# Second weight copies of the mixed tiles in two buffers; group 14's output sum in PSUM tensor PC, added by VectorE after its last chain

## What is computed

```
xn  = layernorm(x)
mixer: x_proj, z = split(xn @ W_in.T);  xc = silu(causal conv over 4 taps + bias)
       dt = softplus(W_dt (W_x[32:] xc) + b_dt);  alpha = sigmoid(dt * 0.1)
       h[l] = clip(alpha) * h[l-1] + (1 - alpha) * B_gate * xc        (256 channels)
       mixer = ((h * C_gate + D * xc) * silu(z)) @ W_out.T
moe:   top 2 of 8 experts by xn @ w_gate, softmax over the two
       expert e: (silu(xn @ w1[e]) * (xn @ w3[e])) @ w2[e]
out = x + mixer + moe
```

## Time and profile before

| | |
|---|---|
| time before, median of 3 runs (lowest to highest) | 471.16 us (471.15 to 471.25) |
| time of the profiled execution | 471.31 us |
| its span | 469.6 us |
| PE, DVE, POOL, ACT busy | 430.6, 388.1, 310.6, 287.7 us |
| mean granted clock of PE | 0.993 |
| full tiles | up to about 371.6 us |
| mixed tiles 31 to 34, and tile 35 | about 371.6 to 405 us |
| tail | from about 405 us |

### The profile page before, as it was taken

One profiled execution on the slowest core, in us unless ns is written; L12 is line 12 of the kernel. 1 busy time (PEld: TensorE's weight loads), 2 busy tenths in 40 slices (PEclk: granted clock), 3 DMA queues, 4 the chain that ended last, 5 costly groups with the idle time before them and its releaser, 6 DMA issues.

```text
span 469.6 us, 8332 instructions
## 1 busy us (share of the span) xinstructions
PE 430.6 (92%) x2440; PEld 308.0 (66%) x2440; DVE 388.1 (83%) x774; ACT 287.7 (61%) x406; POOL 310.6 (66%) x344
## 2 busy tenths in 40 slices
PE   0888999999999999998999999999999878998877
PEld 0777544555554455555888888988988878664446
DVE  5885897999999999996998997677677675399985
ACT  2774469788888988898454434434434433668850
POOL 4677777777777775750677777777777777764200
PEclk9998999999999999999999999999999999999999
DMA  8961117131121312143677756666656652029994
GB/s 239 292 195 45 53 52 239 46 98 54 56 88 52 97 50 82 47 136 98 201 202 239 224 172 198 187 184 177 175 170 190 182 143 85 15 46 266 209 211 121
DMA packets 48077, 65.92 MB, mean 140 GB/s; under 512 B 8424, under 2 KB 30223, under 8 KB 48048
## 3 DMA queue, kind: packets, MB, share of 16 engines
q1 hardware_dynamic: 36240, 39.56, 30.2%
q0 software_dynamic: 10656, 24.47, 18.6%
q10 hardware_dynamic: 1152, 1.57, 1.2%
HBM read 42.09 MB, written 33.83 MB: 162 GB/s over the span
## 4 chain that ended last, share of the span: by engine, by line
PE 48%; DVE 29%; issue 13%; ACT 8%; DMA 1%; DVEq 0%; SPq 0%; ACTq 0%
PE PD L897 13%; DVE hbuf L1404 6%; PE PB L729 4%; DVE hbuf L1415 4%; PE PD L840 3%; PE PB L859 3%; PE PB L863 3%; PE PB L860 3%; PE PA L859 3%; DVE gbuf L1386 3%; PE PA L863 3%; PE PA L860 3%; DVE y L1424 2%; DVE gbuf L1292 2%; PE PC L744 2%
## 5 line engine op out<-in xcount | busy, mean ns | idle before, releaser
L612 POOL DMA_INDIRECT moe_out<-xnT,dst_u x142 | 146.6, 1033 | 61.7 <-issue 37.8
L597 POOL DMA_INDIRECT moe_in<-xn,slot_u x128 | 133.0, 1039 | 44.4 <-issue 39.9
L897 PE MATMUL PD<-xnT,xn 128*128 128x128 f32 x536 | 66.0, 276 | 1.3 <-DVE xn L1630 1.2
L897 PEld LDWEIGHTS PD<-xnT,xn 128*128 128x128 f32 x536 | 62.7, 192 | 2.4 <-DVE xn L1630 2.0
L744 PE MATMUL PC<-xc,Wc 128*128 128x512 f32 x128 | 57.8, 594 | 2.9 <-ACT xc L1102 2.9
L1176 ACT ACTIVATE whi<-xnT 128x512 fp32r<-128x512 f32 x36 | 22.8, 633 | 61.3 <-PE PB L863 61.3
L1205 ACT ACTIVATE xn<-PA 128x1024 f32<-128x1024 f32 (+1 forms) x36 | 36.5, 1013 | 34.4 <-PE PA L863 20.2
L757 PE MATMUL PA<-xnT,Wtap 128*128 (+4 forms) x128 | 57.2, 590 | 0.0
L1630 DVE TENSOR_TENSOR xn<-xn,PB 128x1024 f32<-128x1024 f32 (+1 forms) x36 | 43.4, 1207 | 11.1 <-PE PB L863 9.0
L1623 DVE TENSOR_TENSOR xlo<-PD,xhi 128x512 fp32r<-128x512 f32 (+1 forms) x36 | 24.6, 682 | 27.6 <-ACT xhi L1199 27.6
L757 PEld LDWEIGHTS PA<-xnT,Wtap 128*128 128x128 f32 x128 | 24.3, 190 | 30.5 <-issue 30.5
(11 more groups left out here) (246 smaller groups left out, 916.9 us busy)
## 6 DMA issues: line engine op xcount, KB each, us to landing
xnT<-moe_w SPq DMA_DIRECT2D x36, 256.0 KB
xn<-moe_in SPq DMA_DIRECT2D x31, 266.0 KB
out_dram<-moe_out POOLq DMA_DIRECT2D x12, 512.0 KB, 16.3
xnT<-moe_w SPq DMA_DIRECT2D x36, 128.0 KB
out_dram<-xacc SPq DMA_DIRECT2D x7, 512.0 KB, 3.5
moe_out<-xnT,dst_u POOLq DMA_INDIRECT x142
moe_in<-zrow SPq DMA_DIRECT2D x8, 266.0 KB, 3.4
moe_w<-in_L_ffn_w_dram SPq DMA_DIRECT2D x2, 1024.0 KB
```

The lines of the kernel that those rows point to most:

```text
L597: gp.indirect_dma_start(xs_dram, bass.IndirectOffsetOnAxis(ap=slot_u[:, k, j:j + 1], axis=0), xn_row[:, j, :], None).then_inc(s_scat, 16)
L612: gp.indirect_dma_start(yt_dram, bass.IndirectOffsetOnAxis(ap=dst_u[:, t, j:j + 1], axis=0), yo[t % OUTS][:, j, :], None, bounds_check=lim ...
L897: last = pe.matmul(PD[:, 512 + j * D:512 + (j + 1) * D], hid[b][:, k * SLOTS + j * P:k * SLOTS + (j + 1) * P], (w2x[t - FULL] if mixed and ...
```

## The change

`whix` and `wlox` get two buffers each, used in turn; `round_mixed` and `low_mixed` of the second mixed tile no longer wait, and those of the third and fourth wait for the PB matmuls of one tile earlier than before. On DVE `low_mixed(t+1)` stands ahead of `glu(t)` instead of behind it. In the tail, group 14's sums go to PC instead of PB: PE waits for `softplus(15)` (`s_dt`) instead of `add_out(15)` before them, the eight matmuls into PC and their wait are gone, and the wait before the last group's rows is for `add_out(15)` instead of `add_out(16)`. DVE's `add_out(16)` reads PC and stands behind the last chain part, ahead of the two last sums.

```diff
@@ -127,8 +127,8 @@
         wlo = sb("wlo", [P, 2, 2 * HID], F32R)
-        whix = sb("whix", [P, 2 * HID], F32R)
-        wlox = sb("wlox", [P, 2 * HID], F32R)
+        whix = sb("whix", [P, 2, 2 * HID], F32R)
+        wlox = sb("wlox", [P, 2, 2 * HID], F32R)
         xhi = sb("xhi", [P, 2, SLOTS], F32R)
@@ -868,7 +868,8 @@
                 pe.wait_ge(s_xhi, t + 1)
-                hi, lo = (whi[:, b, :], whix[:, :]), (wlo[:, b, :], wlox[:, :])
+                x = max(t - FULL, 0) % 2
+                hi, lo = (whi[:, b, :], whix[:, x, :]), (wlo[:, b, :], wlox[:, x, :])
                 pe.wait_ge(free, t)
@@ -959,21 +960,18 @@
             out(g, g % SLOT3, True)
-            pe.wait_ge(s_add, g)
             pe.wait_ge(s_rows, 16 * TOP_K)
-            pe.matmul(PB[:, 0:GROUP], ident[:, :], last_rows[0][:, 0:GROUP], start=True, stop=False)
-            pe.matmul(PB[:, 0:GROUP], ident[:, :], last_rows[1][:, 0:GROUP], start=False, stop=False)
+            pe.wait_ge(s_dt, GROUPS)
+            for c in range(TOP_K):
+                pe.matmul(PC[:, 0:GROUP], ident[:, :], last_rows[c][:, 0:GROUP], start=(c == 0), stop=False)
             pe.wait_ge(s_y2, g)
...
                 for k in range(HALVES):
-                    last = pe.matmul(PB[:, j * D:(j + 1) * D], gated_y(g)[:, k, j * P:(j + 1) * P], WoT[:, k, :],
+                    last = pe.matmul(PC[:, j * D:(j + 1) * D], gated_y(g)[:, k, j * P:(j + 1) * P], WoT[:, k, :],
                                      start=False, stop=(j == GT - 1 and k == HALVES - 1))
...
-            pe.wait_ge(s_ch, (GROUPS - 1) * CHAIN + 5)
-            for _ in range(8):
-                pe.matmul(PC[:, 0:P], ident[:, :], ident[:, :], start=True, stop=True)
-            pe.wait_ge(s_add, GROUPS)
+            pe.wait_ge(s_add, g)
             for h in range(2):
@@ -1178,9 +1176,9 @@
                 act.wait_ge(s_w13x[m], 16)
-                if m:
-                    act.wait_ge(s_h3, t)
-                act.activation(whix[:, :], w13x[m], ACT.Copy).then_inc(s_whix, 1)
+                if m > 1:
+                    act.wait_ge(s_h3, t - 1)
+                act.activation(whix[:, m % 2, :], w13x[m], ACT.Copy).then_inc(s_whix, 1)
@@ -1492,14 +1490,14 @@
-            def add_out(g, col=0):
+            def add_out(g, col=0, ps=PB):
...
                 at = bass.ds(g * GT - 2 * GT, GT) if not static else slice((g - 2) * GT, (g - 1) * GT)
-                ve.tensor_tensor(xacc[:, at, :], PB[:, col:col + GROUP].rearrange("p (j d) -> p j d", j=GT),
+                ve.tensor_tensor(xacc[:, at, :], ps[:, col:col + GROUP].rearrange("p (j d) -> p j d", j=GT),
                                  xacc[:, at, :], ALU.add).then_inc(s_add, 1)
@@ -1639,10 +1637,11 @@
             def low_mixed(t, b):
-                ve.wait_ge(s_whix, t - FULL + 1)
-                if t > FULL:
-                    ve.wait_ge(s_h3, t)
-                ve.tensor_tensor(wlox[:, :], w13x[t - FULL], whix[:, :].bitcast(F32), ALU.subtract).then_inc(s_wlox, 1)
+                m = t - FULL
+                ve.wait_ge(s_whix, m + 1)
+                if m > 1:
+                    ve.wait_ge(s_h3, t - 1)
+                ve.tensor_tensor(wlox[:, m % 2, :], w13x[m], whix[:, m % 2, :].bitcast(F32), ALU.subtract).then_inc(s_wlox, 1)
@@ -1703,9 +1702,9 @@
                     sum_p(t + 1, 1 - b, early and t == 0)
-                glu(t, b, early)
                 if isinstance(t, int) and is_mixed(t + 1):
                     low_mixed(t + 1, 1 - b)
+                glu(t, b, early)
@@ -1764,9 +1763,9 @@
             chain(g, slot, 2)
-            add_out(g)
             chain(g, slot, 3)
             chain(g, slot, 5)
+            add_out(g, 0, PC)
```

## The result

The changed kernel takes 466.76 us (median of 4 runs, 466.24 to 467.28) against 471.21 us (4 runs) for the kernel before: ratio 0.9907, 95% interval 0.9891 to 0.9923. It is faster by 4.4 us. The forecast was 464.5 us with a range up to 466.6; the time lies 2.3 us above the one and 0.2 us above the other. The profiled execution took 466.26 us, its span is 464.5 us.

What follows compares the result with a forecast made beforehand. PE, stopped for `wlox` in mixed tiles, and a tail chain mostly through DVE and ACT were taken as bounds; 471.31 - 5.7 (tiles) - 2.6 (tail) + 1.7 (slow clock) = 464.7, as median 464.5 us, range 462.9 to 466.6.

Steps and rivals of the forecast that it cites:

- What bounds: PE runs full tiles without a gap; each of four mixed tiles (6.55 us) stops 1.2 us for `wlox`; POOL late by itself.
- part 1: Mixed tiles: without the wait for `wlox` a tile takes 5.11 us instead of 6.55; 5.7 us saved, bounds 4.8 to 5.8.
- the ring through DVE and ACT: Mixed tiles: chain from one gate through xhi, `scale_y`, `wlox` and `glu` to the next, about 5.1 us, level with PE's 5.11.
- (b): Mixed tiles: DVE and ACT decide at 5.4 us a tile, or SP's row loads do; saving 4.7, total 465.5 us; chance 0.12.
- (d): Mixed tiles: the wait becomes an equal one for `glu` or `hid`, so only the tail's change works: 470.2 us; chance 0.05.
- (e): Tail: `add_out(14)` waits for the second transfer onto `xacc`, making it slower; landing at 450 gives 473.6 us; chance 0.03.
- Part 2: Tail, group 14 in PC: work starts 2.60 us earlier; PE's last 16 instructions at half clock take 1.7 us more.
- the 2.60: Tail: L1409 begins at 458.69 plus 0.03 instead of 461.32, since `add_out(16)` moves back: 2.60 us earlier.
- rival (a): Tail: PE's clock does not fall before the last matmuls, or only for the last few: 463.2 us; chance 0.17.
- forecast place: Tail: the last sum was to start at 465.95 - 5.7 = 460.25 us.
- Does something hold the tail?: Tail transfers: queue ends at 458 to 460, `add_out(14)` has 2.7 us of margin; no cost taken, bound 0 to 1.5 us.
- Rival (c): Kernel's end: final stores land up to 1.5 us late, or the queue ends at 462: 465.5 to 466.5 us; chance 0.11.

Runs made afterwards that it cites:

- two separate edits of POOL's end: Changed kernel with the last wait for the accumulating transfers on SP instead of POOL: 464.89 us; changed kernel without its last accumulating transfer: 464.79 us (both chip A).
- the changed kernel with SP's waits: Against the changed kernel, the last wait for the twelve accumulating transfers onto the output stands on SP, not POOL: 464.89 us, ratio 0.9871 (chip A).

## Why the prediction was wrong

**What bounds, and part 1: right.** The wait for `wlox` is gone, a tile takes 5.11 us as forecast, and the ring through DVE and ACT shows only as late gates on ACT. From tile 31's start to group 12's L744 it was 401.69 - 371.61 = 30.08 us and is 394.73 - 370.29 = 24.44: 5.64 us against the 5.7 taken. For comparison, the row of before:

```profile
401.69 1.88 PE L744 MATMUL PC<-xc,Wc 128*128 128x512 f32 x4
```

Rivals (b) and (d) fell with that. `add_out(14)` is at 439.6 and waits for no transfer: (e) fell too.

**Part 2: the mechanism right, its size taken from an execution whose clock fell.** L1407 stands straight behind the scan, `add_out(16)` costs nothing, PE idles 3.58 us (forecast 3.6). The forecast for this stretch was 15.50 - 2.60 + 1.7 = 14.6 us; it was 13.97, since the clock fell only within L984, which took 1.05 us more instead of 1.7. But the 2.60 held 1.7 us of slow clock of the old tail, and of six traces of the old tail only the profiled one has that. That does not make it rare: of the kernel before's eight executions on chip A two have the mean clock of the profiled one, 0.993, three have 0.996 and three 1.000. The prediction treated the fall as a property of the kernel; the runs show it in some executions of a kernel and not in others, and what rival (a) says of the clock holds in four of the new tail's nine traces. The Trainium skill, "TensorE: Matmul & The Clock Gate", section "HAM oscillation — how this bites in real kernels", has the burst behind each long wait begin cold; here, behind the same wait of 3.57 to 3.58 us, it was granted full speed throughout in four traces and 0.50 for most of it in five. The same holds at 36 us, where the profile of before fell and that of after did not: 1.3 us of their difference, ahead of all that was changed. So of the 1.9 us by which the last sum beat its forecast place, 1.3 came from the clock there and 0.6 from the clock in L984.

**The step that failed: "Does something hold the tail?"**, with "I take no cost, bound 0 to 1.5 us". It asked when POOL's queue would end and put that at 458 to 460 us, which is where it ended (458.5). It did not ask what POOL does then. Its DRAIN of 5.63 us stood in the trace of before, at 461.8, hidden by 1.9 us, and the forecast moved the computation's end by 5.7 + 2.6 - 1.7 = 6.6 us and POOL's queue by 2.5 at most. Measured, SP's end moved 8.2 us (469.3 to 461.1) and POOL's 3.2 (461.8 to 458.6), so 1.9 us of cover became 3.1 us of excess. From the prediction's own terms: 458 to 460, plus 5.63, plus 0.3 to the end of the span, is 463.9 to 465.9; with 1.7 around it 465.6 to 467.6 us. Measured 466.76. The last sum came 1.9 us earlier than forecast, but since POOL decides, the time does not show it.

Rival (c), "the transfers hold the end", named the right engine's work and by luck nearly the time (465.5 to 466.5), but through late stores or a queue that ends at 462, and neither happened: the last store landed 1.7 us after SP began to wait for it. That two separate edits of POOL's end give back 2.3 to 2.4 us shows the cause.

The cover of 1.9 us is that of the profiled execution: without its two falls of the clock the old kernel's last sum would come at about 466.85 - 1.3 - 1.7 = 463.9 and its span end at 466.6, an estimate, and two of its executions on chip A at clock 1.000 have spans of 467.1 and 467.5. POOL's DRAIN may have held those already; no trace here is of such an execution.

In the two profiled executions the account closes: the last sum is 8.50 us earlier (1.32 by the clock at 36 us, 5.64 by the tiles, 1.53 by the tail, 0.01 between), and from there to the span's end it is 464.5 - 458.35 = 6.15 us instead of 469.6 - 466.85 = 2.75. 8.50 - 3.40 = 5.10 = 469.6 - 464.5.

The best version measured is the changed kernel with SP's waits: 464.89 us, 6.0 us below the kernel before on the same chip.

## What to carry to other kernels

Before a large gain on the path is booked, list for every engine when it is through with its closing instructions, drains included, not only when its last useful work ends: the second latest is the floor, and the change's gain ends there. Where an engine with long transfers waits for them at its end and is the last one, try letting another engine hold that wait: it was worth 2.3 us here. And a clock fall seen in one profile is one draw: price a tail at both clocks before subtracting a slow stretch.

## What the runs showed of the hardware

POOL's DRAIN took 5.63 us in every trace in which POOL had first waited for its last accumulating transfer (5.55 with one transfer fewer), against 0.46 us for DVE's and 0.01 for SP's. Issued right behind the last issue it took 17.8 to 18.4 us and lay over the transfers, and ended some 4 us behind them where that can be seen (535.9 against 532 on chip B, 544.8 against 541 and 543.0 against 539 on chip E). What POOL does in it no trace shows. Between the same kernel's executions the granted clock behind the same idle time differed, which moved the last sum by up to 1.7 us; with fourteen unread matmuls in that time it was full in five traces of five. Without them it was full in two of four on the same chips, so that they keep it full is likely, not shown.
